# A graph network on one core: 28 of 196 edge blocks of layers two and three come as a product of edge counts with node rows

## The reference

```python
h = jnp.maximum(_layernorm(x), 0.0)
deg = segment_sum(ones_like(src), dst, N); inv_deg = 1.0 / maximum(deg, 1.0)
for i in range(3):                                   # relu after the first two
    agg = segment_sum(h[src], dst, N)
    h = h @ W_self[i] + (agg * inv_deg[:, None]) @ W_neigh[i] + b[i]
x = x + h
h = jnp.maximum(_layernorm(x), 0.0)
x = x + attention_and_feed_forward(h, src, dst)      # unchanged by the edit
```

## Time and profile before

| | |
|---|---|
| median of three runs | 4306.53 us |
| the profiled execution, its own time | 4308.08 us, of which 4306.3 us are the span |
| layer one, last sum of tile 48 | at 1023.9 us |
| layer two, last sum of tile 48 | at 2006.2 us |
| layer three, last sum of tile 48 | at 2987.5 us |
| rest: attention, feed-forward | to 4306.3 us |
| busy: TensorE, GpSimd, VectorE, ScalarE | 76%, 70%, 50%, 11% of the span |

### The profile page before, as it was taken

One profiled execution on the slowest core, in us unless ns is written; L12 is line 12 of the kernel. 1 busy time (PEld: TensorE's weight loads), 2 busy tenths in 40 slices (PEclk: granted clock), 3 DMA queues, 4 the chain that ended last, 5 costly groups with the idle time before them and its releaser, 6 DMA issues. The chain is left out here.

```text
span 4306.3 us, 75198 instructions
## 1 busy us (share of the span) xinstructions
PE 3277.9 (76%) x13728; PEld 2372.7 (55%) x13729; DVE 2147.4 (50%) x6078; ACT 487.8 (11%) x1111; POOL 3020.7 (70%) x3154
## 2 busy tenths in 40 slices
PE   3777777777777777777788778887777777776798
PEld 2565555555555555555566555565655555555544
DVE  6434333333333333333455555545577777777733
ACT  4000000000000000000011101101011111111122
POOL 5777777777777777777777777776777777777200
PEclk9888889898888888888999999999888889898999
DMA  6444434435344344344444444445655555554411
GB/s 202 121 136 124 124 106 124 125 105 143 105 125 125 105 125 124 106 125 127 130 140 136 142 136 136 142 135 155 162 147 157 148 159 147 157 146 138 127 60 60
DMA packets 284796, 563.69 MB, mean 131 GB/s; under 512 B 104638, under 2 KB 176133, under 8 KB 279691
## 3 DMA queue, kind: packets, MB, share of 16 engines
q0 software_dynamic: 150528, 414.45, 34.0%
q10 hardware_dynamic: 70180, 89.46, 6.3%
q1 hardware_dynamic: 63974, 58.59, 4.4%
HBM read 487.19 MB, written 73.45 MB: 130 GB/s over the span
## 5 line engine op out<-in xcount | busy, mean ns | idle before, releaser
L763 POOL DMA_INDIRECT arena<-h_table,idx_v x2292 | 2174.3, 949 | 726.3 <-issue 694.0
L895 PE MATMUL banks<-arena 128*128 x5856 | 1544.9, 420 | 617.9 <-SPq L790 506.0
L895 PEld LDWEIGHTS banks<-arena 128*128 128x128 f32 x5856 | 1171.5, 208 | 957.2 <-issue 774.4
L842 DVE TENSOR_SCALAR arena<-iota_t,dst_e 128x128 f32<-128x128 f32 x2928 | 846.8, 310 | 821.7 <-PE banks L895 575.9
L1278 POOL DMA_INDIRECT arena<-vs_table,idx_v x764 | 765.0, 1001 | 232.8 <-issue 228.8
L1496 PE MATMUL banks<-arena 128*128 x1952 | 518.8, 416 | 52.8 <-DVE arena L1840 52.6
L1496 PEld LDWEIGHTS banks<-arena 128*128 128x128 f32 x1952 | 366.5, 199 | 192.5 <-issue 120.4
L916 PE MATMUL banks<-arena,lhs 128*128 128x256 f32 x1176 | 339.6, 439 | 5.0 <-ACT lhs L1016 0.2
L948 DVE TENSOR_SCALAR small<-banks 128x1 f32<-128x1 f32 x147 | 23.2, 158 | 638.7 <-PE banks L897 638.7
L1016 ACT ACTIVATE lhs<-banks 128x512 f32<-128x512 f32 x147 | 87.8, 597 | 2073.7 <-PE banks L907 2073.5
L916 PEld LDWEIGHTS banks<-arena,lhs 128*128 128x128 f32 x1176 | 240.5, 215 | 100.8 <-ACT lhs L1016 64.8
(11 more groups left out here) (263 smaller groups left out, 2468.4 us busy)
## 6 DMA issues: line engine op xcount, KB each, us to landing
arena<-h_table,idx_v POOLq DMA_INDIRECT x2292
arena<-dst_dram SPq DMA_DIRECT2D x14, 1792.0 KB
arena<-vs_table,idx_v POOLq DMA_INDIRECT x764
h_table<-arena ACTq DMA_DIRECT2D x11, 1024.0 KB, 7.4
h_early<-arena ACTq DMA_DIRECT2D x10, 1024.0 KB
vs_table<-arena ACTq DMA_DIRECT2D x49, 132.0 KB
x_dram<-arena ACTq DMA_DIRECT2D x49, 128.0 KB
hln_dram<-arena ACTq DMA_DIRECT2D x49, 128.0 KB
```

The lines of the kernel that those rows point to most:

```text
L763: pool.indirect_dma_start(ring[:, s * BJ + j, 0:width], None, table, bass.IndirectOffsetOnAxis(idx_v[:, half, n * BJ + j:n * BJ + j + 1], ...
L842: dve.tensor_scalar(onehot[:, j, :], iota_t[:], dst_e[:, bass.ds(b * BJ + j, 1)], None, ALU.is_equal).then_inc(W["onehot_made"], 1)
L895: pe.matmul(agg[:, 0:D + 1], onehot[:, j, :], ring[:, (b % SLOTS) * BJ + j, 0:D + 1], start=False, stop=False).then_inc(W["onehot_used"], 1)
```

## The change

Of the 196 blocks, 28 are chosen on the chip (of every seven the fourth, and where it has more than 41 destination nodes, `COUNT_W`, another). For these the kernel counts, once, how many edges lead from each node to each of the block's 41 destinations. The counts stand in 49 slices (one for every 128 source nodes) of [128 x 1148] int16 in HBM (1148 = 28 x 41). In layers two and three the chosen blocks are not gathered. In their place the layer before adds up, slice by slice, (counts of the slice, turned) x (rows of the slice, `h_nodes`) in five banks of PSUM, 9 products of 128 x 128 x 256 per slice (`fold_tensor`). The 1148 sums are copied behind the ring as three further blocks (`folded_rows_vector`), and are treated as edges with a destination of their own.

What follows from it in the program:

- **Counts**, in layer one in tiles 8 to 23, after the steps of the tile, two blocks behind three tiles and one behind the fourth: per quarter block VectorE makes a one-hot of 128 and one of 2016 columns in bf16, TensorE multiplies them in four matmuls, and per block ScalarE copies [128 x 2009] from PSUM to int16.
- **Folds**: in layer one two slices after each of the tiles 25 to 47; in layer two one slice after each tile. ScalarE turns a slice to fp32 (`counts_scalar`) ahead of the tile's steps and issues the load of the slice after the next.
- **Tables**: `pick_tables_vector` with 62 steps after tile 4, the attention's tables after tile 2 instead of 7, `late_ends` after tile 6 instead of 15; the four DMAs of `batch_tables_scalar` after tile 7 instead of behind layer one, with a wait for their landing.
- **Layers two and three** sum, for each tile, first the pairs with the three further blocks (3 + 48 pairs), then those with the 168 gathered ones (168 + 48), in two loops, each with two register loads (`span_of`). The degree isn't summed again; the reciprocals of layer one are kept (`inv_deg`).

```diff
+        def count_block_vector(dve, i):
+            for j in range(BJ):
+                at = bass.ds(i * BJ + j, 1)
+                dve.wait_ge(counted, i * BJ + (COUNTED + j - 1))
+                dve.tensor_scalar(low_hot[j % 2], count_iota[:, 0:P], count_low[:, at], None, ALU.is_equal).then_inc(coded, 1)
+                dve.tensor_scalar(count_hot[j % 2], count_iota, count_code[:, at], None, ALU.is_equal).then_inc(coded, 1)
+        def count_block_tensor(pe, i):
+            pe.wait_ge(counts_taken, i + TAKEN)
+            for j in range(BJ):
+                pe.wait_ge(coded, i * (2 * BJ) + (CODED + 2 * j + 2))
+                for n in range(0, HOT_W, BE):
+                    to = min(n + BE, HOT_W)
+                    last = pe.matmul(banks[:, 4 + n // BE, 0:to - n], low_hot[j % 2], count_hot[j % 2][:, n:to], start=j == 0, stop=j == BJ - 1)
+                last.then_inc(counted, 1)
+        def counts_scalar(act, l, m, half, more=True):
+            s = m * 2 + half
+            act.wait_ge(counts_in[half], ...)
+            act.wait_ge(counts_used, s + (COUNTS_USED + l * NT - 1))
+            act.activation(counts[half], counts16[half], ACT.Copy).then_inc(counts_ready, 1)
+            if more:
+                act.wait_ge(counts_ready, s + (READY + l * NT + 1))
+                counts_load(act, s + 2, half)
+        def fold_tensor(pe, l, m, half):
+            s = m * 2 + half
+            pe.wait_ge(W["h_made"], since("h_made", l, s + 1))
+            pe.wait_ge(counts_ready, s + (READY + l * NT + 1))
+            for c in range(CSLOTS):
+                n = min(P, CCOLS - c * P)
+                last = pe.matmul(banks[0:n, 3 + c // 2, c % 2 * D:c % 2 * D + D], counts[half][:, c * P:c * P + n], h_nodes[:, s, :],
+                                 start=False, stop=False)
+            last.then_inc(counts_used, 1)
...
+        def span_of(eng, t, h):
+            both = eng.value_load(span2[0:1, bass.ds(t * 2 + h, 1)], min_val=0, max_val=NX * NX - 1)
+            off = eng.value_load(offset2[0:1, bass.ds(t * 2 + h, 1)], min_val=0, max_val=PAIRS2)
+            return both % NX, both // NX, off
+        def onehots2(dve, w, t, between=None):
...
+            b0, b1, off = base_of_tile(dve, w, t)
+            with dve.Fori(b0, b1 + 1) as b:
+                of_block(b, off)
+            if between is not None:
+                between()
+            b0, b1, off = span_of(dve, t, 1)
+            with dve.Fori(b0, b1 + 1) as b:
+                of_block(b, off)
...
@@ sage_tensor, layer one
-                first_and_rest(pe, 2 * GS, step)
+                step(0)
+                steps(1, PICK_AT)
+                pick_tables_tensor(pe)
+                steps(PICK_AT, LATE_AT)
                 late_ends_tensor(pe)
-                with pe.Fori(2 * GS, NT) as t:
+                steps(LATE_AT, COUNT_FROM)
+                with pe.Fori(0, COUNT_GROUPS) as q:
+                    for r in range(4):
+                        step(q * 4 + (COUNT_FROM + r))
+                        for c in group_blocks(r):
+                            count_block_tensor(pe, q * COUNT_GROUP + c)
...
+                with pe.Fori(FOLD_FROM, NT - 1) as t:
                     step(t)
+                    fold_tensor(pe, 0, t - FOLD_FROM, 0)
+                    fold_tensor(pe, 0, t - FOLD_FROM, 1)
...
@@ sage_vector, means
-                dve.tensor_scalar(small[:, 0:1], agg[:, D:D + 1], 1.0, None, ALU.max).then_inc(W["deg"], 1)
-                dve.reciprocal(small[:, 1:2], small[:, 0:1]).then_inc(W["deg"], 1)
+                if l == 0:
+                    dve.tensor_scalar(small[:, 0:1], agg[:, D:D + 1], 1.0, None, ALU.max).then_inc(W["deg"], 1)
+                    dve.reciprocal(inv_deg[:, bass.ds(t, 1)], small[:, 0:1]).then_inc(W["deg"], 1)
```

More of the change, by code:

```diff
@@ new lines, in fold_close, with folded_rows_vector @@
+        def fold_close(pe):
+            for i in range(3, 8):
+                last = pe.matmul(banks[:, i, :], zeros[:, 0:P], zeros[:], start=False, stop=True)
+            last.then_inc(folded, 1)
+        def folded_rows_vector(dve, l):
+            dve.wait_ge(folded, FOLDED + l)
+            if l == 1 and CSLOTS < NV * BJ:
+                dve.memset(ring[:, SLOTS * BJ + CSLOTS:(SLOTS + NV) * BJ, 0:D], 0.0).then_inc(rows_folded, 1)
+            dve.tensor_copy(ring[:, SLOTS * BJ:SLOTS * BJ + CSLOTS, 0:D],
+                            banks[:, 3:8, :].rearrange("p b n -> p (b n)")[:, 0:CSLOTS * D].rearrange("p (c d) -> p c d", d=D)
+                            ).then_inc(rows_folded, 1)
@@ L774, in relay @@
             if w == 0:
[L775 to L776 removed]
                 sp.sem_inc(W["slots_free"], SLOTS)
+            else:
+                sp.wait_ge(tables_made, PICKED)
             def free(n):
[L780 removed]
+                sp.wait_ge(W["onehot_used"], since("onehot_used", w, (pairs_of if w == 0 else pairs2_of)(sp, n)))
                 sp.sem_inc(W["slots_free"], 1)
@@ L1066, in sage_scalar @@
                 store(0, GS)
-                if l == 0:
-                    late_setup_scalar(act)
+                late_setup_scalar(act)
+                batch_tables_scalar(act)
+                act.wait_ge(marks_out, 64)
+                with act.Fori(1, 3) as g:
+                    with act.Fori(g * 2 - 2, g * 2) as q:
+                        for r in range(4):
+                            step(q * 4 + (COUNT_FROM + r))
+                            for c in group_blocks(r):
+                                count_block_scalar(act, q, c)
+                        counts_store(act, q)
+                    store(g * GS, GS)
@@ new lines, in sage_scalar @@
+                step(FOLD_FROM - 1)
+                act.wait_ge(counts_out, COUNTS_OUT + 16 * COUNT_GROUPS)
+                for half in range(2):
+                    counts_load(act, half, half)
+                with act.Fori(FOLD_FROM, 4 * GS) as t:
+                    with_counts(t)
+                store(3 * GS, GS)
+                with act.Fori(4 * GS, 5 * GS) as t:
+                    with_counts(t)
+                store(4 * GS, GS)
+                with act.Fori(5 * GS, NT - 2) as t:
+                    with_counts(t)
@@ new lines, in sage_scalar @@
+                store(NT - 1 - GS, GS - 1)
+                with_counts(NT - 2)
+                store(NT - 2)
+                counts_scalar(act, 0, NT // 2 - 1, 0)
+                counts_scalar(act, 0, NT // 2 - 1, 1, False)
+                counts_scalar(act, 0, NT // 2, 0, False)
+                step(NT - 1)
+                store(NT - 1)
+            elif l == 1:
+                act.wait_ge(counts_ready, READY + NT)
+                for half in range(2):
+                    counts_load(act, half, half)
+                step(0)
+                counts_scalar(act, 1, 0, 0)
+                step(1)
+                with act.Fori(1, GS // 2) as m:
+                    two_with_counts(m)
+                store(0, GS)
```

392 lines of the change are left out of this document (348 added, 44 removed).

## The result

The change makes the kernel slower: 4622.65 us median of four runs against 4306.27 of the kernel before, ratio 1.0726 (95% interval 1.0705 to 1.0747). The prediction was 4329 us, 4240 to 4385. One run of the four took 10801 us, and the ratio leaves it out. The profiled execution took 4622.03 us, of which 4620.2 are the span: 314 us more than the one before.

The account below looks back on a forecast made before the run. GpSimd's gathers were taken to bound the kernel. Early tiles +49, counts +45, folds +8, borders +5 and +11, layer two -102 and layer three +7 make +23 us: a median of 4329 us, range 4240 to 4385.

Parts of the forecast that it names:

- What bounds the kernel, and the possible gain: GpSimd's gathers set the pace; 135 us less in each of two layers, only where TensorE and VectorE keep up.
- Layer three: VectorE's loads delay the list part, TensorE idles and its clock drops: 20.0 us a tile, +7 us.
- My rival at GpSimd's pace: Layer three at 17.2 to 18.8 us a tile if sequencers do loads while engines work: 4243 us; chance 0.26.
- Layer two: TensorE at 17.7 us a tile, GpSimd at 17.1: 949.2 us become 847, -102 us.
- Counts: Layer one, tiles 8 to 23: counting delays TensorE's sums, 22.7 us a tile for 19.7 before, +45 us.
- The port: Count phase: gathers lose 0.3 to 0.4 us per fast one-hot; GpSimd stays just under TensorE's 22.7 us, costing nothing.
- The rival's 1.7 us: Mean gather time beside the counts if the port decides that phase, +45 us: 4374 us; chance 0.12.
- Folds: Layer one, tiles 25 to 47: two slices a tile, 21.1 us for 20.0, +8 us over the stretch of 480.8.
- Early tiles: Layer one: tables of 40 us on VectorE and ScalarE's 37 us of issues make tile 9 close 49 us later.
- Borders: Two more slices, closing and a copy, 12 us: +5 us into layer two, +11 us into layer three.

Follow-up runs that it names:

- m1: i1 with TensorE's two loops told apart, less register work at its block border, its offset worked out each turn; 4232.42 us, 0.983 of the kernel before.
- f3: The kernel before with two idle register loads more on VectorE in layer three, behind the normalization; 4315.89 us.
- f1: The changed kernel with two loads instead of four at a tile's head in layer three, and the counts' store in two parts; 4478.41 us.
- f2: The changed kernel with VectorE's loads where it waits anyway, counts stored in 28 KB pieces, the tables' landing wait earlier; 4345.42 us, 1.0075 of the kernel before.
- g1: f2 with TensorE's span loads at a tile's head and, in layer three, VectorE's first one-hots ahead of the mean; 4330.29 us, 1.0055 of the kernel before.
- g2: g1 with ScalarE issuing the late weights' and tables' transfers after tile 4 instead of 7; 4306.48 us, 1.0002 of the kernel before.
- i1: g2 with a tile's two offsets worked out once into registers on VectorE and TensorE instead of in each loop turn; 4313.16 us.

## Why the prediction was wrong

*What bounds the kernel, and the possible gain.* Right. GpSimd's pace set the kernel before, and what 28 blocks less give (135 us a layer; 130 between the marks, 48 x 2.7) is had only where TensorE and VectorE keep up: m1 gets 119 us of it in layer three and 68 in layer two.

*Layer three: +7 forecast, +137 measured.* The mechanism stood in the prediction (VectorE's loads, TensorE's idling, the lower clock), with a size too small in every term. The list part starts 12.8 us behind the mark, not 11.8: two loads ahead of the first one-hots cost 1.0 us and not 0.4, two behind the normalization 1.6 and not 1.3. The clock was put at 0.6 us from a row in which TensorE had idled 2.68 us; behind the 3.2 to 3.5 us here it costs about 1.9: 34.8 records at 0.284 us instead of 0.229, the pace of the changed kernel at full clock. The rest is that pace: the prediction read 24 records as 5.1 us, which is from the first start to the last and thus 23 of them. So 22.7 us a tile, 2.7 above the forecast and 2.1 outside its bound of 20.6. f3 shows loads and clock alone, f1 and f2 that they go when the loads go. My rival at GpSimd's pace had the loads hidden by the sequencers; they are not, on VectorE.

*Layer two: -102 forecast, -30 measured.* The first sums were right within 0.2 us. Of the 1.5 us a tile that were missed, 0.5 are the pace of a pair (1.86 us for 1.77), read from a loop whose border has less register work. 0.3 are TensorE's loads between its two loops, put at 0.3 us "since it reads ahead" and 0.6 in the trace, since the 8 records of one block do not cover two loads, and six gaps are near 2 us. 0.5 are the waits for rows that SyncE declares late, which stood in no term: 19 us in the layer, and still 17 in m1. The last 0.1 is in the addition, whose terms make 17.8 and not 17.65. The bound of 18.6 did not hold 19.15 either. g1 shows the loads' term and m1 the border's; what makes the few long gaps and what makes SyncE late was not tried.

*Counts: +45 forecast, +94 measured.* The tile without a store was right (17.8 to 25.1 us, and f2's 340.2 us from tile 9 to 24 are the forecast's 22.7 a tile to the digit). The store was left out of the sum. It was in the diff, its landing was waited for, and behind it on the same queue stood the rows' store. By f2, which stores in wide pieces, it costs 49 us here and 12 more among the folds (tile 25 takes 32.0 us for 16.4, and tile 26 gives 4 of them back).

*The port.* The gathers from 270 to 700 us take 1.03 us on average, for 0.95 behind that, and those beside a fast one-hot 1.23: 0.18 us per one-hot, where 0.3 to 0.4 was put; with TensorE the slower of the two, no time is seen to hang on it, as forecast. The rival's 1.7 us did not come.

*Folds: +8 forecast, +35 measured.* The price of a tile was right: 21.0 us for 21.1 over the 23 tiles with folds. Two things were not: the store costs 12 us here, and my sum was wrong by 15, since 23 tiles of 21.1 us are 485.3 and left 3.5 us for tile 25 (480.8 + 8 - 485.3), where f2, without the wait, needs 504.2 for the stretch.

*Early tiles: +49 forecast, +68 measured.* The tables took 46.2 us for 40; the ring covered 19 us of them (150.97 to 170.13) and not 30, since the tables at tile 3 had emptied part of it; ScalarE's stall was right (40.5 for 37, landing 9 us for 8). g2 shows that the two stalls add.

*Borders.* Right within 3 us.

The step that failed is thus layer three's term, 130 of the 291 us by which the sum is off: what VectorE's serial work and TensorE's idling behind it cost. Next come layer two's with 72, for the most part by the same kind of serial work on TensorE and by rows declared late, and the store, 61 us, that stood in no term.

## What to carry to other kernels

When an engine that bounds a kernel is relieved, price the next one's serial chain with register loads, loop borders and divisions in full, and ask where the engine behind it will idle, since idling may be paid again in clock. Put the loads where the engine waits anyway. And look at every new transfer for what stands behind it on its queue: here a large one in small pieces held up the issue of the next. Where a profile says which engine ended a wait, look also at who declared the data ready just before.

## What the runs showed of the hardware

- A register load on VectorE is not hidden behind its engine's work: two loads in an otherwise unchanged kernel moved the next one-hots by 1.4 us (f3).
- TensorE's granted clock stood at 1.00 behind 1.7 us of idling, and at 0.65 and 0.56 in the 3.8 us behind 3.5 and 3.2 us of it, between its levels of 2.4 and 1.2 GHz; that cost 1.7 us in a kernel in which only the idling had changed (f3).
- The issue of a 1 MB transfer took 23.7 us behind a 3.5 MB store in pieces of 574 bytes on the same queue, and 18.5 behind 1.5 MB in as many pieces (f1). With 28 KB pieces ScalarE did not wait (f2).
- A gather of GpSimd beside one of VectorE's fast bf16 one-hots (0.74 us) took 1.23 us, and 0.95 beside none.
- 0.2 us less of register work at a block's border on TensorE's queue was worth 0.14 to 0.2 us a block, and 71 us in two layers (m1 against i1).
